# The seam between an FFN phase and a scan phase: who prepares the scan's first weights, rows and parameters, and where the last norm stands

## The reference, cut

```python
x = _layernorm(x + _L0_attn_ref(x, ...))        # attention, 16 heads
x = _layernorm(x + _L0_ffn_ref(x, ...))         # two branches of 8 experts, running sums; no gain, no bias in this norm
x = _layernorm(x + _L1_attn_ref(x, ...))        # the scan, below
x = _layernorm(x + _L1_ffn_ref(x, ...))         # top 2 of 20 experts

def _L1_attn_ref(u, log_A, D_skip, dt_bias, W_dt, b_dt, W_B, b_B, W_C, b_C):
    A = -jnp.exp(log_A)
    dt = jax.nn.softplus(u @ W_dt.T + b_dt + dt_bias)
    Bt = (u @ W_B.T + b_B).reshape(b, l, d, n)
    Ct = (u @ W_C.T + b_C).reshape(b, l, d, n)
    A_bar = jnp.exp(dt[..., None] * A)
    x_in = (A_bar - 1.0) / A * Bt * u[..., None]
    # h = A_bar * h + x_in over the tokens;  y = sum over n of Ct * h, plus D_skip * u
```

## Time and profile before

| | |
|---|---|
| median of 3 runs | 2469.5 us (2467.14 to 2472.96) |
| the profiled execution's own time | 2470.99 us |
| its span, first to last instruction | 2469.0 us |
| mean granted TensorE clock | 0.982 of full speed |
| busy time PE, DVE, ACT, POOL | 2328.9, 1922.0, 1425.2, 1049.3 us |
| FFN's last output ends, scan's first matmul starts | 1487.09, 1505.90 us |

### The profile page before, as it was taken

The page is one execution under the profiler, slowest core; times in us unless marked ns, Lnnn a source line. Parts: engine busy times, 40 slices in busy tenths (PEclk is TensorE's granted clock), DMA queues, the critical chain, the costliest instruction groups (busy, mean ns, idle before and its releaser), DMA issues. The chain is left out here.

```text
span 2469.0 us, 40630 instructions
## 1 busy us (share of the span) xinstructions
PE 2328.9 (94%) x13523; PEld 1500.3 (61%) x13523; DVE 1922.0 (78%) x4359; ACT 1425.2 (58%) x2608; POOL 1049.3 (42%) x1032
## 2 busy tenths in 40 slices
PE   8999999999999998899999997999999999999992
PEld 5433333333333333577777775888888777887782
DVE  3888888888888881556666656999999989898366
ACT  3477667676667666445454535666565676654420
POOL 3512221111221211100011004999999877898364
PEclk9999999999999999999999998999999999999996
DMA  8643222224322202100000001111111222224794
GB/s 256 176 71 77 52 52 52 52 56 68 82 52 52 52 22 76 61 9 26 19 25 18 9 18 44 52 65 52 65 58 58 71 104 68 73 74 151 225 330 154
DMA packets 111766, 190.04 MB, mean 77 GB/s; under 512 B 15956, under 2 KB 74120, under 8 KB 108360
## 3 DMA queue, kind: packets, MB, share of 16 engines
q1 hardware_dynamic: 84328, 150.22, 23.0%
q10 hardware_dynamic: 21088, 20.45, 2.4%
q0 software_dynamic: 6144, 16.79, 2.1%
HBM read 104.13 MB, written 78.79 MB: 74 GB/s over the span
## 5 line engine op out<-in xcount | busy, mean ns | idle before, releaser
L627 ACT ACTIVATE ssm_in_dt<-att_s 128x512 f32<-128x512 f32 (+3 forms) x1280 | 600.3, 536 | 258.0 <-PE att_s L537 185.0
L537 PE MATMUL att_s<-att_qs,att_ks 64*128 64x512 f32 (+3 forms) x1280 | 444.5, 422 | 27.0 <-ACT ssm_in_dt L627 25.3
L524 PE MATMUL att_s<-att_ks,att_qs 64*128 64x512 f32 (+3 forms) x1280 | 441.9, 424 | 5.9 <-DVE ssm_in_u L761 4.0
L537 PEld LDWEIGHTS att_s<-att_qs,att_ks 64*128 64x128 f32 x1280 | 208.4, 184 | 367.8 <-ACT ssm_in_dt L627 325.1
L1941 PE MATMUL ssm_ps<-ssm_hi,ssm_halves 128*128 128x512 f32 x1024 | 407.1, 398 | 14.2 <-DVE ssm_lo L2399 7.1
L1943 PE MATMUL ssm_ps<-ssm_hi,ssm_halves 128*128 128x512 f32 x1024 | 401.2, 392 | 0.0
L1942 PE MATMUL ssm_ps<-ssm_lo,ssm_halves 128*128 128x512 f32 x1024 | 401.2, 392 | 0.0
L2332 POOL TENSOR_TENSOR ssm_cc<-ssm_cc,ssm_h 128x512 f32<-128x512 f32 x256 | 332.7, 1300 | 74.7 <-DVE ssm_h L2428 64.4
L2341 POOL TENSOR_TENSOR ssm_out_z<-ssm_out_z,ssm_cc 128x512 f32<-128x512 f32 x256 | 339.0, 1324 | 0.1
L448 POOL TENSOR_SCALAR_AFFINE_SELECT ssm_in_dt<-ssm_in_dt 128x256 f32<-128x256 f32 x256 | 104.6, 409 | 543.8 <-ACT ssm_in_dt L627 531.9
L570 PE MATMUL att_o_ps<-ssm_in_dt,att_vst 128*32 128x512 f32 (+3 forms) x2560 | 299.8, 540 | 2.4 <-ACT ssm_in_dt L627 0.8
(11 more groups left out here) (333 smaller groups left out, 3631.8 us busy)
## 6 DMA issues: line engine op xcount, KB each, us to landing
qk_halves<-ssm_in_dt SPq DMA_DIRECT2D x64, 256.0 KB, 3.0
scan_halves<-ssm_halves SPq DMA_DIRECT2D x32, 512.0 KB, 2.9
ssm_halves<-scan_halves SPq DMA_DIRECT2D x32, 512.0 KB, 3.5
moe_sorted<-att_hidden SPq DMA_DIRECT2D x31, 512.0 KB, 9.6
moe_answers<-ssm_cc ACTq DMA_DIRECT2D x62, 256.0 KB, 3.9
att_stage_q<-qk_halves SPq DMA_DIRECT2D x96, 128.0 KB, 4.4
att_stage_k<-qk_halves SPq DMA_DIRECT2D x96, 128.0 KB, 6.0
ssm_raw<-in_w_bc SPq DMA_DIRECT2D x30, 256.0 KB, 3.3
```

Source lines behind the costliest of these rows:

```text
L524: mm = nc.tensor.matmul(s1[:, S1_BANK[at], 0:hi - lo], qs[p % 3][half(b), I * P:(I + 1) * P], ks[p % 3][half(b), lo:hi], start=True, stop= ...
L537: mm = nc.tensor.matmul(s2[:, turn % RING, 0:hi - lo], ks[p % 3][half(b), J * P:(J + 1) * P], qs[p % 3][half(b), lo:hi], start=True, stop= ...
L627: nc.scalar.activation(prob[:, b, step % 2, x * CH + lo:(x + 1) * CH], s2[:, turn % RING, 0:CH - lo], ACT.Exp, scale=1.0 / HD).then_inc(s2 ...
```

## The change

The change does four things.

- A stack of buffers, `t.seam`, is opened ahead of the FFN phase and closed after the scan. It holds the rounded rows of two chunks (`row_hi`, `row_lo`), the rounded weights of two blocks (`block`), `par`, the skip and the step-size bias, and all eight banks. FFN and scan both work in these: the FFN's `hi`, `lo`, `x_hi`, `x_lo` lie in them.
- In the FFN's last chunk ScalarE and VectorE, behind their own work, make the scan's first rounded weights (blocks 0 and 1), the rounded rows of chunks 0 and 1, and the parameters.
- The last chunk's residual rows are loaded straight into their place in `u_sb` (`t.last_rows`). The norm of their first half (tiles 0, 1) is done in the FFN, that of the second half (tiles 2, 3) at the head of the scan.
- The turning of these rows and their step sizes are moved among the scan's first units: `turn_last` behind unit 1, `size_last` behind units 2 and 3, in plain float32 with two matmuls each instead of six rounded ones; `keep_last` and `bias_last` on ScalarE. The softplus pieces of chunk 7 move to units 5 to 15.

```diff
+    t.seam = ExitStack()
+    sp = Space(nc, t.seam, "seam")
+    t.row_hi, t.row_lo = ([sp.sb(f"{part}{c}", [P, KT, CH], F32R) for c in range(ROUNDED)] for part in ("hi", "lo"))
+    t.block = [sp.sb(f"block{m}", [P, 2, KT, 2 * P], F32R) for m in range(KT)]
...
@@ FFN, SyncE: load_res(c)
-                else:
+                elif c < LAST:
                     filled(eng, c, ("x2T", KT - 1))
-                eng.dma_start(res[:], x1[:]).then_inc(res_loaded, 16)
+                eng.dma_start(t.last_rows if c == LAST else res[:], x1[:]).then_inc(res_loaded, 16)
@@ FFN, TensorE, behind chunk 7
-            emptied(eng, LAST, ("w", NG - 1))
-            for k in range(KT):
-                turn_x2(BEYOND, k)
-            for m in range(KT):
-                step_size(BEYOND, m)
@@ FFN, ScalarE, behind chunk 7
-            deviation(BEYOND)
-            read_x2(BEYOND)
-            add_bias(BEYOND)
+            filled(eng, LAST, ("w", NG - 1))
+            eng.wait_ge(next_loaded, 16 * 6)
...
+            nc.scalar.copy(t.block[0][:, 0], t.first_w[:, 0]).then_inc(next_hi_ready, 1)
+            nc.scalar.copy(hi[0][:], first_rows[:, 0]).then_inc(next_hi_ready, 1)
+            nc.scalar.copy(hi[1][:], first_rows[:, 1]).then_inc(next_hi_ready, 1)
+            nc.scalar.copy(t.block[1][:, 0], t.first_w[:, 1]).then_inc(next_hi_ready, 1)
+            nc.scalar.activation(t.par[:, 1], t.first_par[:, 0], ACT.Exp).then_inc(par_ready, 1)
+            eng.wait_ge(var_ready, BEYOND)
+            nc.scalar.activation(std[:, 0:2], mv[:, 0:2, 1], ACT.Sqrt, bias=eps[:]).then_inc(std_ready, 1)
@@ FFN, VectorE, behind chunk 7
-            means(BEYOND)
-            normalise(BEYOND)
-            round_x2(BEYOND)
+            rest = lambda out, whole, part: nc.vector.tensor_tensor(out, whole, part.bitcast(F32), ALU.subtract)
...
+            rest(t.block[0][:, 1], t.first_w[:, 0], t.block[0][:, 0])
...
+            rest(lo[0][:], first_rows[:, 0], hi[0][:])
...
+            nc.vector.tensor_tensor(par[:, 4], t.first_par[:, 2], par[:, 2], ALU.mult)
+            eng.wait_ge(res_loaded, 16 * NCH)
+            eng.wait_ge(o_ready, TPC * LAST + 2)
+            two = t.last_rows[:, 0:2]
...
+            softplus(LAST)
+            eng.wait_ge(std_ready, BEYOND)
...
@@ scan
-        BY_POOL = (1, 2)
+        BY_POOL = (2,)
...
+            eng.dma_start(last_w, t.w_dt).then_inc(last_w_loaded, 16)
             for b in range(KT, 2 * KT):
                 load_raw(b)
             eng.dma_start(ident[:], t.ident).then_inc(ident_loaded, 16)
@@ scan, TensorE
+                    if g == 1 and read is c_read:
+                        eng.wait_ge(last_out_read, 1)
...
+            def turn_last():
+
+                eng.wait_ge(ident_loaded, 16)
+                eng.wait_ge(last_normed, 1)
...
+            def size_last(m):
+                if m == 0:
+                    eng.wait_ge(last_w_loaded, 16)
+                    eng.wait_ge(last_kept, 1)
...
+                for k in range(KT):
+                    mm = nc.tensor.matmul(spare, last_w[:, k, m * P:(m + 1) * P], u[:, NCH - 1, k], start=k == 0, stop=k == KT - 1)
...
+                if g == 1:
+                    turn_last()
+                if g in (2, 3):
+                    size_last(g - 2)
@@ scan, ScalarE
-            round_weights(0)
-            round_hi(0)
-            nc.scalar.activation(par[:, 1], t.first_par[:, 0], ACT.Exp).then_inc(par_ready, 1)
-            round_hi(1)
-            eng.wait_ge(last_abs, 1)
-            nc.scalar.activation(t.last_expn, t.last_expn, ACT.Exp).then_inc(last_expn, 1)
-            eng.wait_ge(par_ready, 4)
...
+            eng.wait_ge(last_var, 1)
+            nc.scalar.activation(std[:, NT - 2:NT], mv[:, NT - 2:NT, 1], ACT.Sqrt, bias=eps[:]).then_inc(last_std, 1)
             decay(0)
...
+                if g == 1:
+                    keep_last()
+                    eng.wait_ge(last_kept, 1)
                 if g + 1 < UNITS:
                     decay(g + 1)
...
+                if g in (2, 3):
+                    bias_last(g - 2)
+                if g == 7:
+                    eng.wait_ge(last_abs, 1)
+                    nc.scalar.activation(t.last_expn, t.last_expn, ACT.Exp).then_inc(last_expn, 1)
@@ scan, VectorE
-            round_w(0)
-            round_lo(0)
-            nc.vector.scalar_tensor_tensor(out=t.last_expn, in0=pre, scalar=-1.0, in1=pre, op0=ALU.mult, op1=ALU.min).then_inc(last_abs, 1)
...
+            norm_last()
             driven(0)
             driven(1)
             decayed(0)
...
-                if g == 0:
-                    round_w(1)
+                if g == 5:
+                    minus_abs()
```

More of the change, by code:

```diff
@@ L1259, in round_hi @@
                     filled(eng, c, ("w", NG - 1))
[L1260 removed]
+                nc.scalar.copy(hi[a][:], src[:, a]).then_inc(hi_ready, 1)
             def hidden(c, n):
@@ L1698, in phase_scan @@
     t.halves_bc = nc.dram_tensor("scan_halves", (BLOCKS, P, 2 * KT * 2 * P), F32).ap()
-    with nc.cleanup_on_exit(), ExitStack() as ctx:
+    with t.seam, nc.cleanup_on_exit(), ExitStack() as ctx:
         sp = Space(nc, ctx, "ssm")
@@ L1708, in phase_scan @@
         x3 = z_flat.rearrange("p (n d) -> p n d", d=D)
-        hi, lo = sp.sb("hi", [P, HELD, KT, CH], F32R), sp.sb("lo", [P, HELD, KT, CH], F32R)
-        halves = [sp.sb(f"halves{m}", [P, 2, KT, 2 * P], F32R) for m in range(KT)]
+        hi, lo = (rooms + [sp.sb(f"{part}{c}", [P, KT, CH], F32R) for c in range(ROUNDED, HELD)]
+                  for part, rooms in (("hi", t.row_hi), ("lo", t.row_lo)))
+        halves = t.block
         raw_sb = sp.sb("raw", [P, KT, KT * 2 * P])
@@ L1775, in phase_scan @@
         junk = work[:, 0:2 * D]
+        last_w = work[:, 0:KT * D].rearrange("p (k d) -> p k d", k=KT)
         def xT_of(c):
@@ L1848, in rounded, with weights_ready @@
                 eng.wait_ge(pool_lo_ready, BY_POOL.index(ch) + 1)
-            else:
-                eng.wait_ge(lo_ready, len([c for c in range(ch + 1) if c not in BY_POOL]))
+            elif ch >= ROUNDED:
+                eng.wait_ge(lo_ready, len([c for c in range(ROUNDED, ch + 1) if c not in BY_POOL]))
+        def weights_ready(eng, blocks):
+            after(eng, w_ready, blocks - KT)
         def uses(pairs, s):
```

173 lines of the change are left out of this document (112 added, 61 removed).

## The result

The changed kernel took 2453.49 us (median of 6 runs, 2450.28 to 2459.86) where the kernel before took 2471.23 beside it (6 runs, 2467.14 to 2475.24). The profiled execution took 2455.18 us, its span is 2453.5 (before 2469.0), the mean granted clock 0.985.

The account below looks back on a forecast made before the run. It took TensorE to bound the settled scan, and a chain of waits and half clock the seam. -18.8 to unit 5, +0.8 given back, +1.4 clock make -16.6 us: 2452.9 from the 2469.5 median, range 2449.5 to 2457.5.

Parts of the forecast that it names:

- point (7): Expected profile sign: VectorE without idle time in units 6 to 16, unit 39 17 to 18 us earlier, everything behind shifted whole.
- FFN tail: End of the FFN: the work moved there costs nothing, hidden under TensorE's last outputs with 1.9 us of cover left.
- Handover: Between FFN and scan: the scan starts 0.96 us after TensorE's last FFN output ends.
- Units 0, 1 and the transposes: Scan start: 24 matmuls in 5.45 us, then eight transposes in 1.07, without waits; identity matrix there 4.9 us after start.
- Unit 2: Early scan: waits for GpSimd's rounding behind ScalarE's queue, until 8.85 us after scan start; TensorE idle 2.3 us.
- The table switch: ScalarE's queue ahead of unit 2: a switch behind the root costs 1.31 us, without the skill's extra 1.38 us drain.
- Clock: Scan's first units: one stretch of some 3.4 us at half clock, costing 1.4 us, bounds 0 and 3.
- No half-rate stretch: Rival for the seam: the clock never falls, saving 18.0 us, 2451.5 us; chance 0.26.
- point (6): Expected profile sign: unit 5 about 21.5 us after the last FFN output ended, against 40.2 before.
- Given back later: Behind unit 5: the minus-absolute pass moved among VectorE's scan work costs 0.8 us, bounds 0 and 1.14.

Follow-up runs that it names:

- the added passes: Four unused VectorE passes over 128x1024 added to the changed kernel's last FFN chunk, ahead of the first half's norm; ratio 0.9947 to the kernel before.
- the second trace: The changed kernel run again with nothing changed; ratio 0.9921 to the kernel before.
- the norm-first kernel: The changed kernel with the last rows' transposes and both step-size products put back ahead of unit 0; ratio 0.9964 to the kernel before.

## Why the prediction came out right, step by step

The forecast was -16.6 us, the measurement -16.3 (by the medians 2452.9 against 2453.49). The sum is better than its terms, for two errors of some 2 us cancel, and that is luck. In the traces: FFN -2.1 (not forecast), E to unit 5 -16.7 (forecast -17.4, clock included), unit 5 to 60 +3.0 (forecast +0.8): -15.9 together. Unit 39 starts 13.8 us sooner behind E, where point (7) said 17 to 18.

*FFN tail: right.* VectorE ended 1.9 us ahead of TensorE (1483.64 against 1485.52), as forecast, and the added passes measured that cover. The small products took 0.19 us where nothing runs beside them.

*Handover: right,* 1.00 for 0.96 us.

*Units 0, 1 and the transposes: right in what they cost,* but not in the identity matrix. It was reckoned to be there at S + 4.9 and landed at S + 5.8 and 6.1, 4.5 and 4.8 us behind its issue and not 3.4. TensorE stood 0.13 and 0.44 us for it, paid out of unit 2's wait.

*Unit 2: right,* S + 9.01 and 9.02 for S + 8.85, released by GpSimd's rounding behind ScalarE's queue, TensorE idle 2.10 us for 2.3. Taking the cast out of that queue took the wait away.

*The table switch: right.* In the changed kernel the root ends at 1488.73, and this follows on ScalarE:

```profile
1488.43 0.30 ACT L2316 ACTIVATE moe_std<-moe_mv,moe_eps 128x2 f32<-128x2 f32 x1 [7.80 <-DVE moe_mv L2729]
1488.74 1.28 ACT L2196 ACT_TABLE_LOAD   x1
1490.04 1.30 ACT L2196 ACTIVATE seam_banks<-ssm_in_dt,seam_par 128x512 f32<-128x512 f32 x2
```

0.01 us lies between the root's end and the load, and 1.30 between the load's start and the decay's. The rule of the Trainium skill ("ScalarE: Activation LUTs", What ACT_TABLE_LOAD costs), 2.66 us for a switch, does not hold here.

*Clock: right in size; whether it falls changes from one execution to the next.* One stretch of 3.4 us costs 1.63 us by the two traces of one program; forecast 1.4. "No half-rate stretch", a rival with 0.26, happened in the second trace, where unit 5 came 21.78 us behind E; point (6) had said 21.5, without the stretch.

*Given back later: the term that was mis-sized,* +0.8 (bounds 0 and 1.14) against +3.0. It priced the minus-absolute pass by its row in the seam, where GpSimd stood idle; among the units it took 2.26 us. And it took the later pieces as free since they "only move one unit"; that shift cost 0.8. The other 2.2 us are what is left over: the backlog that the pass leaves and, by the norm-first kernel for about 1 us, how the first units run. Point (7) of what was to be seen, everything shifted as a whole from unit 6 on, was wrong by these 3 us.

*What offset it* was the FFN, 2.1 us shorter for a reason that stays open and that no step of the prediction named.
